# Row maximum in twelve one-bank parts, and a new order inside the attention chunk

## What is computed

```python
xn = _layernorm(x, axis=-1)
# attention: x 4 x 1024 x 128, 16 heads of 64
normed = xn / l2 * dim ** 0.5 * gamma
qkv = (normed @ w_qkv).reshape(b, n, 3, h, d)
sim = jnp.einsum('bhid,bhjd->bhij', q * d ** (-0.5), k)
sim = jnp.where(causal_mask, mask_value, sim)
attn = jax.nn.softmax(sim, axis=-1)
out = jnp.einsum('bhij,bhjd->bhid', attn, v)      # then @ w_out
# experts: top 2 of 8, relu(xn @ W1 + b1) @ W2 + b2, weighted, then layer_norm(xn + sum)
x = x + attention(xn) + experts(xn)
```

## Time and profile before

| | value |
|---|---|
| median of three runs | 1487.04 us |
| the profiled execution | 1485.95 us, span 1484.2 us |
| TensorE busy | 1396.8 us (94%) |
| VectorE busy | 1104.8 us (74%) |
| ScalarE busy | 1058.7 us (71%) |
| GpSimd busy | 947.7 us (64%) |
| attention stage | from about 262 us to the end |
| TensorE waits for row_max at L1271, all of the run | 20.8 us |
| TensorE waits for p_lo at L1313, all of the run | 1.3 us |
| one exponential (L1075), mean | 490 ns |
| VectorE's reductions (L1123), all 512 | 385.9 us |
| mean granted clock of TensorE | 0.975 |

### The profile page before, as it was taken

How to read it: one execution, slowest core, us unless ns; L and a number is a source line. 1 busy time by engine, 2 the same in 40 slices (tenths; PEclk the granted TensorE clock), 3 DMA queues, 4 the chain that set the end, 5 groups by cost and what they waited for, 6 DMA issues and landing times.

```text
span 1484.2 us, 27052 instructions
## 1 busy us (share of the span) xinstructions
PE 1396.8 (94%) x8618; PEld 1069.1 (72%) x8618; DVE 1104.8 (74%) x1928; ACT 1058.7 (71%) x2589; POOL 947.7 (64%) x933
## 2 busy tenths in 40 slices
PE   3689999599999999999999999999999999999996
PEld 3679999367777777777777777777777777777774
DVE  6645555458876987698769876987688768876985
ACT  2556666377777777777777777777777777777774
POOL 1774000168667866786678667866786678667775
PEclk9689999799999999999999999999999999999998
DMA  9122221122212221221122212221212121212112
GB/s 328 63 89 64 68 58 51 39 49 53 49 44 59 53 51 43 59 55 47 44 62 53 50 41 63 51 49 43 63 51 49 44 62 50 49 44 62 50 44 75
DMA packets 77226, 89.89 MB, mean 61 GB/s; under 512 B 17656, under 2 KB 54816, under 8 KB 77088
## 3 DMA queue, kind: packets, MB, share of 16 engines
q1 hardware_dynamic: 59168, 69.90, 18.6%
q10 hardware_dynamic: 13824, 9.86, 2.1%
q0 software_dynamic: 4096, 8.40, 2.0%
HBM read 37.25 MB, written 16.78 MB: 36 GB/s over the span
## 4 chain that ended last, share of the span: by engine, by line
PE 58%; DVE 11%; POOL 6%; issue 4%; ACT 2%; DMA 1%; SPq 0%; POOLq 0%
PE max_ps L1271 9%; PE head_ps L1313 7%; PE head_ps L1315 7%; PE head_ps L1317 7%; PE score_ps L1297 7%; PE score_ps L1296 6%; DVE row_max L1123 4%; POOL p_lo L1037 4%; PE misc_ps L1247 3%; PE misc_ps L1327 3%; POOL two_y L1030 2%; PE max_ps L1274 2%; PE misc_ps L1241 2%; PE score_ps L1299 2%; PE misc_ps L1243 2%
## 5 line engine op out<-in xcount | busy, mean ns | idle before, releaser
L1037 POOL TENSOR_TENSOR p_lo<-probs,p_hi 128x512 fp32r<-128x512 f32 (+3 forms) x768 | 805.5, 1068 | 322.5 <-ACT p_hi L1075 317.5
L1075 ACT ACTIVATE probs<-score_ps 128x512 f32<-128x512 f32 (+3 forms) x768 | 376.5, 490 | 211.8 <-PE score_ps L1299 116.7
L1123 DVE TENSOR_REDUCE row_max<-max_ps 128x1 f32<-128x128 f32 (+7 forms) x512 | 385.9, 754 | 174.0 <-PE max_ps L1274 169.0
L1075 ACT ACTIVATE p_hi<-score_ps 128x512 fp32r<-128x512 f32 (+3 forms) x768 | 375.3, 489 | 0.0
L1313 PE MATMUL head_ps<-p_hi,v_hi 128*65 128x512 f32 (+3 forms) x768 | 289.3, 377 | 2.2 <-POOL p_lo L1037 1.3
L1271 PE MATMUL max_ps<-k_a,q_a 128*128 128x384 f32 (+5 forms) x768 | 259.8, 393 | 26.2 <-DVE row_max L1123 20.8
L1296 PE MATMUL score_ps<-q_a,k_a 128*128 128x512 f32 (+3 forms) x768 | 266.5, 347 | 2.5 <-DMA q_b<-shift 2.5
L1297 PE MATMUL score_ps<-q_b,k_b 65*128 65x512 f32 (+3 forms) x768 | 267.7, 349 | 0.0
L1317 PE MATMUL head_ps<-p_lo,v_hi 128*65 128x512 f32 (+3 forms) x768 | 258.8, 337 | 0.0
L1315 PE MATMUL head_ps<-p_hi,v_lo 128*64 128x512 f32 (+3 forms) x768 | 258.7, 337 | 0.0
L1296 PEld LDWEIGHTS score_ps<-q_a,k_a 128*128 128x128 f32 x768 | 144.9, 189 | 45.2 <-issue 3.4
(11 more groups left out here) (162 smaller groups left out, 2193.6 us busy)
## 6 DMA issues: line engine op xcount, KB each, us to landing
k_a<-k_a SPq DMA_DIRECT2D x64, 256.0 KB, 4.0
q_b<-q_a SPq DMA_DIRECT2D x64, 256.0 KB, 4.8
scale<-inv_rows SPq DMA_DIRECT2D x128, 128.0 KB, 2.9
sorted_x<-zeros SPq DMA_DIRECT2D x13, 384.0 KB, 16.4
sorted_y<-result ACTq DMA_DIRECT2D x78, 64.0 KB, 1.7
w_raw<-sorted_x SPq DMA_DIRECT2D x25, 192.0 KB, 2.5
acc<-in_L_attn_x_dram SPq DMA_DIRECT2D x4, 512.0 KB, 6.9
w_raw<-in_L_ffn_W_dram ACTq DMA_DIRECT2D x1, 2048.0 KB, 23.2
```

Source lines behind the costliest of these rows:

```text
L1037: pool.tensor_tensor(p_lo[:, slot, 0:w], probs[:, n_chunk(g, c) % PROBS, 0:w], p_hi[:, slot, 0:w].bitcast(F32), ALU.subtract).then_inc(p_s ...
L1075: ins = act.activation(p[:, n_chunk(g, c) % ring, 0:width], score_ps[n_chunk(g, c) % 2][:, 0:width], ACT.Exp, scale=SCALE)
L1123: dve.tensor_reduce(row_max[:, g % 2, t:t + 1], src, axes, ALU.max).then_inc(max_taken, 1)
```

## The change

- The row maximum of a head comes in twelve parts, each in one bank, one part a chunk. A wide tile is two parts of half its width, whose results go to two columns of `row_max` (now `TILES + GROUP` wide). After the last part one small `tensor_tensor` maximum joins the four pairs (`max_merged`), and the shift of the second half waits for that. Part m waits for the reduction of part m - 2.
- Inside a chunk the order is: score, the first two weighted products, the maximum, the third weighted product (`pv_low`), then projection, `y` and shift. Before, it was score, maximum, projection, `y`, shift, and all three weighted products. The first two now wait for `probs_ready` (ScalarE), the third for `p_split` (GpSimd).
- `PROJECT_AT`, `COMBINE_AT`, `Y_AT` and the tables of the first head are moved to suit.
- The last step of a combine waits for the additions of `y` before it.
- In the expert stage TensorE keeps the expert's number of a tile in its register instead of reading it again two steps later.

```diff
@@ expert stage, TensorE
-                            inside = i is not None
-                            e_out = tile_experts[k - 2] if inside else expert_of(pe, j - 2)
+                            e_out = tile_experts[j - 2]
@@ tables
-            row_max = sb(ph2, "row_max", [P, 2, TILES])
+            row_max = sb(ph2, "row_max", [P, 2, TILES + GROUP])
-            max_parts = [(0, 0), (1, 1), (2, 0), (3, 1), (7, None), (6, None), (5, None), (4, None)]
-            MAX_AT = [0, 1, 2, 3, 5, 7, 10, 11]
-            FIRST_WIDE = {0: (4, 5), 1: (6,), 2: (7,)}
-            FIRST_MAX_AT = [3, 4, 5, 6, 7, 8, 9, 10]
+            max_parts = [(t, 0, (t + 1) * P, True) for t in range(4)]
+            for t in (7, 6, 5, 4):
+                w = (t + 1) * P // 2
+                max_parts += [(t, 0, w, False), (t, w, w, True)]
+            MAX_AT = {c: (c,) for c in range(CH)}
+            FIRST_WIDE = {0: (4, 5, 6), 1: (7, 8, 9), 2: (10, 11)}
+            FIRST_MAX_AT = {3: (0, 1), 4: (2,), 5: (3,), 6: (4, 5), 7: (6,), 8: (7, 8), 9: (9, 10), 10: (11,)}
-            BEFORE = [-1, -1, 0, 1, 3, 4, 5, 6]
-            HALF_MAX = [3, PARTS - 1]
+            NARROW = 4
-            PROJECT_AT = [{1: 0, 2: 1, 3: 2, 5: 3, 6: 4, 10: 5}, {}]
+            PROJECT_AT = [{1: 0, 2: 1, 4: 2, 5: 3, 6: 4, 9: 5}, {}]
-            COMBINE_AT = [(g, c) for g in (3, 4, 5, 6, 7) for c in (0, 1, 4, 6, 8, 9, 10, 11)][:COMBINE_STEPS]
-            Y_AT = {11: 0, 22: 1}
+            COMBINE_AT = [(g, c) for g in (3, 4, 5, 6, 7) for c in (0, 1, 3, 7, 8, 9, 10, 11)][:COMBINE_STEPS]
+            Y_AT = {11: 0, 17: 1}
@@ beside(at)
+                values = at >= LAG and (at - LAG) // CH < ALL_HEADS
+                if values:
+                    order.append(("pv", (at - LAG) // CH, (at - LAG) % CH))
                 max_at = MAX_AT if g else FIRST_MAX_AT
                 if g + 1 < ALL_HEADS and c in max_at:
-                    order.append(("max", g + 1, max_at.index(c)))
+                    order += [("max", g + 1, m) for m in max_at[c]]
+                if values:
+                    order.append(("pv_low", (at - LAG) // CH, (at - LAG) % CH))
...
-                if at >= LAG and (at - LAG) // CH < ALL_HEADS:
-                    order.append(("pv", (at - LAG) // CH, (at - LAG) % CH))
@@ VectorE, maximum(g, m)
-                        t, bank = max_parts[m]
+                        t, k0, w, _ = max_parts[m]
+                        to = t + GROUP if k0 else t
                         dve.wait_ge(max_scores, n_max(g, m) + 1)
...
+                        dve.tensor_reduce(row_max[:, g % 2, to:to + 1], max_ps[:, m % 2, 0:w], AX_X,
+                                          ALU.max).then_inc(max_taken, 1)
+                        if m == PARTS - 1:
+                            dve.wait_ge(max_taken, n_max(g, m) + 1)
+                            dve.tensor_tensor(row_max[:, g % 2, GROUP:TILES], row_max[:, g % 2, GROUP:TILES],
+                                              row_max[:, g % 2, TILES:TILES + GROUP], ALU.max).then_inc(max_merged, 1)
@@ VectorE, last step of combine
+                            if added[0]:
+                                dve.wait_ge(y_added, added[0] + 2)
@@ TensorE, max_scores_of(g, m)
+                        if n_max(g, m) >= 2:
+                            pe.wait_ge(max_taken, n_max(g, m) - 1)
+                        ins = pe.matmul(max_ps[:, m % 2, 0:w], q_a[i][s][:, t * P:(t + 1) * P],
+                                        k_a[i][s][:, k0:k0 + w], start=True, stop=not diagonal)
+                        if diagonal:
+                            ins = pe.matmul(max_ps[:, m % 2, w - P:w], later[:], ident16[:], start=False, stop=True)
@@ TensorE, shifts(g, half, u)
-                        pe.wait_ge(max_taken, n_max(g, HALF_MAX[half]) + 1)
+                        if half:
+                            pe.wait_ge(max_merged, g + 1)
+                        else:
+                            pe.wait_ge(max_taken, n_max(g, NARROW - 1) + 1)
@@ TensorE, values(g, c), and the new low_values(g, c)
-                        pe.wait_ge(p_split, n_chunk(g, c) + 1)
+                        pe.wait_ge(probs_ready, n_chunk(g, c) + 1 + 2)
...
+                    def low_values(g, c):
...
+                        pe.wait_ge(p_split, n_chunk(g, c) + 1)
                         pe.matmul(head_ps[0:HEAD + 1, cols], v_hi[i][:, j, s], p_lo[:, slot, 0:width],
                                   start=False, stop=c in LAST).then_inc(pv_done, 1)
```

More of the change, by code:

```diff
@@ L736, in attention_and_experts @@
         max_taken = sem("max_taken")
+        max_merged = sem("max_merged")
         misc_ready = sem("misc_ready")
@@ L904, in attention_and_experts @@
             order = [(kind, 0, n) for n in range(6) for kind in ("project", "project_lo")]
-            order += [("max", 0, m) for m in range(HALF_MAX[0] + 1)] + [("shift", 0, 0)]
+            order += [("max", 0, m) for m in range(NARROW)] + [("shift", 0, 0)]
             for at in range(ALL_HEADS * CH + 2 * CH):
@@ L1084, in _ @@
                             shifts(g, c, u)
-                        elif kind == "pv" and c in LAST:
+                        elif kind == "pv_low" and c in LAST:
                             half = LAST.index(c)
@@ L1116, in maximum @@
                     def maximum(g, m):
-                        t, bank = max_parts[m]
+                        t, k0, w, _ = max_parts[m]
+                        to = t + GROUP if k0 else t
                         dve.wait_ge(max_scores, n_max(g, m) + 1)
[L1119 to L1123, removed]
+                        dve.tensor_reduce(row_max[:, g % 2, to:to + 1], max_ps[:, m % 2, 0:w], AX_X,
[4 more added lines that the diff above has]
+                                              row_max[:, g % 2, TILES:TILES + GROUP], ALU.max).then_inc(max_merged, 1)
                     summed = [0]
+                    added = [0]
                     def combine(hp, part):
@@ L1188, in add_y @@
                                           acc[:, toks], ALU.add).then_inc(y_added, 1)
+                        added[0] += 1
                     dve.sem_inc(pv_done, RING)
@@ L1252, in max_scores_of @@
                         i, s = g // 2 % 2, g % 2
-                        t, bank = max_parts[m]
+                        t, k0, w, diagonal = max_parts[m]
                         if m == 0 and s == 0:
@@ L1316, in values @@
                                   start=False, stop=False)
+                    def low_values(g, c):
+                        half, j, q0 = chunks[c]
+                        i, s = g // 2 % 2, g % 2
+                        width = (half + 1) * BANK - q0
+                        slot, cols = (g * CH + c) % RING, slice(q0, (half + 1) * BANK)
+                        pe.wait_ge(p_split, n_chunk(g, c) + 1)
                         pe.matmul(head_ps[0:HEAD + 1, cols], v_hi[i][:, j, s], p_lo[:, slot, 0:width],
@@ L1341, in _ @@
                             values(g, c)
+                        elif kind == "pv_low":
+                            low_values(g, c)
                         elif kind == "y":
```

## The result

The changed kernel takes 1499.24 us, the median of four runs (1498.15 to 1500.89), against 1487.01 before. The ratio is 1.0088, with a 95% interval of 1.0067 to 1.0109: slower by 12 us, where 1455 was forecast. Its profiled execution took 1498.15 us, 12.2 more than that of before.

A forecast was written before the change was run, and what follows sets the result against it. TensorE's own time was taken to bound the attention stage, VectorE second. From 1485.95 us, 26 for 7.5 periods of eight heads and 5 for the experts were subtracted, giving 1455; range 1430 to 1480.

The forecast's parts named there:

- The load order: TensorE, attention heads: narrow products get narrower loads behind them, saving 0.55 us per even and 0.30 per odd head.
- rival B: TensorE in attention: reordering weight loads gives nothing, only head 6 falls, to 22.1 us; total 1476; chance 0.18.
- The expert stage: TensorE no longer rereads the expert's number in 78 steps: 0.06 us a step, 5 us, between 0 and 6.
- VectorE's share: VectorE per head: split reductions add 0.63 us, small maximum 0.5; in all 1.15, between 0.8 and 1.85.
- The waits: TensorE waiting in attention: head 6's wait goes, VectorE's lag partly remains; eight heads take 144.1 us, saving 3.5.
- Moving combine, projection and output steps: Attention heads' step tables: changes no sum; the output projection waits only if VectorE lags over some 2.5 us.
- The shift's chain: Row-maximum transpose in chunks 0 and 8 to its score product: nothing lost, 0.9 us of cover.
- C: Rival, slower: VectorE sets heads 3, 4 and 6 and keeps its idle time; total 1507 us; chance 0.12.

## Why the prediction was wrong

**The load order** was right. The floors came out at 19.74 and 15.35 us, for 20.0 and 15.2. An even and an odd head save 0.81 and 0.17 against 0.55 and 0.30 forecast, 0.98 a pair against 0.85; so the pair is right and its split is not. By itself it is worth 19 us, which puts rival B out: under it, the order alone would have given nothing.

**The expert stage** was right in kind and too small: steps take 2.14 us in place of some 2.24, the stage is 7.4 us shorter, and the register alone gives 9 us in the total, where 5 was taken and 6 was the bound. Some 2 us of the 9 are less half clock in the first head, as the register's own run shows. The bound failed because the transposes behind a copy can start earlier than the quick step of the earlier trace rows showed: 0.12 us after it, for 0.15. These are two neighbouring steps of the changed kernel, with the copy of the first:

```profile
170.56 0.69 DVE L604 COPY w_raw<-bank 128x512 f32<-128x512 f32 x1
...
171.37 0.60 PE L707 MATMUL bank<-ident,w_raw 128*128 128x128 f32 x4
...
173.50 0.60 PE L707 MATMUL bank<-ident,w_raw 128*128 128x128 f32 x4
```

**VectorE's share** holds the step that failed. The split reductions were a little cheaper than said: 417.9 us in 768 against 385.9 in 512, 0.50 us a head for 0.63. The small maximum was put at 0.5 us, with one whole subtraction of GpSimd, 1.07, as the upper end. It took 1.1 us on average and 3.75 at most. The upper end was wrong because it took for granted that the small maximum is let in after one subtraction. In most places it is: outside head 2's end it takes 0.73 us on average. At the end of head 2 it isn't: it is held through three whole subtractions and ends with the last of them. Besides, 1.07 is the mean over four widths; in the kernel before, a subtraction of 512 columns lasts 1.30. The Trainium skill (SBUF — State Buffer, Who interferes with whom) has the rule that bears on it: an operation of VectorE with two SBUF inputs contends with one of GpSimd that reads SBUF, and `tensor_reduce` never does on trn2. The runs agree, with 161 to 3746 ns against 160 to 165. I had cited the lock in the prediction and taken too small a price from it.

**The waits.** The wait of head 6 went, as said: that head takes 20.71 us, for 21.8 forecast. A new one came at the transpose of chunk 0, where the prediction looked for it, but in 40 heads of 64 and for 37.4 us: 2.04 us in head 3, 0.54, 0.77, 0.85 and 0.38 in heads 2, 4, 6 and 7. The second mistake is here. I gave the small maximum's price to VectorE's total and then let TensorE's slack absorb most of it, head by head. But the operation lies on the shift's chain. Between the last reduction and the moment when TensorE reaches the transpose there are 1.9 us in head 3 and none in head 4, and what the operation takes beyond that is TensorE's at once. VectorE's free time doesn't help: it had 28 us in eight heads before, and has 22 after. The four short falls of the clock behind head 3's wait, 6 us, weren't in the sum at all.

**Moving combine, projection and output steps** was said to change no sum. It costs 6 to 7 us in the twelve-part kernel. Which of the three tables does it was not tried.

**The shift's chain** itself was priced right: with the one-operand maximum added to it in eight parts, it costs nothing.

**The rivals.** C was on the right side, with the wrong place and a wrong reason for the size: its head 6 at 24.5 us came out at 20.71, and its head 2 at 20.6 came out at 21.83. The chance of 0.12 for C was too low for an operation that the trace of before didn't show and that stood on a chain.

**The rest of the sum.** With the second operand gone the changed kernel takes 1463.4 us, 8 above 1455. That it comes so near is partly luck, because two errors cancel. These are heads 2 and 4 and the sum of that kernel's eight heads:

```profile
609.37:631.23 21.86, 20.55 (x129) 15.06 (x127) 18.03 (x29) 17.75 (x40) 20.74 (x21) 1.00 0.34 83
...
646.58:668.88 22.30, 20.59 (x128) 14.86 (x127) 21.55 (x38) 17.87 (x40) 13.66 (x14) 1.00 0.32 76
...
sum 146.04, PE 142.27 PEld 104.75 DVE 124.41 ACT 114.82 POOL 107.92; mean PE 17.78 PEld 13.09 DVE 15.55 ACT 14.35 POOL 13.49
```

Forecast were 20.1, 20.8 and 144.1. In head 2 TensorE waits 1.1 us for GpSimd's subtractions, a wait that the prediction put at nothing; in head 4 it waits 1.7 for VectorE. The heads behind the first gain 12 us in all, where 26 were taken. On the other side, the first score product comes 9.3 us earlier and the first head is 2.1 shorter, where 5 were taken.

## What to carry to other kernels

A tiny VectorE operation with two SBUF inputs costs what GpSimd is doing, not its own size: here the rest of a subtraction in most places, and three whole ones in a row in one. Where something waits for it, use a form with one SBUF input (a reduction over a strided view, or an operand in PSUM), or keep it off the chain. Where two weight loads differ in width, put the narrow load behind the narrow product; that was worth 19 us here with no instruction saved. An operation that the trace doesn't show yet deserves a price in its worst place, one place at a time, before it is averaged over the program.

## What the runs showed of the hardware

Pauses of TensorE in the middle of dense work are sometimes followed by a short fall of its clock. Head 3 of the period that begins with head 8 in the changed kernel has the same instructions as the head 3 above (17.54 us at 1.00), and takes 19.07:

```profile
490.88:509.95 19.07, 17.04 (x101) 12.29 (x100) 15.04 (x24) 11.04 (x27) 12.53 (x13) 0.91 0.05 16
```

A clock of 0.91 over this stretch is 1.2 GHz instead of 2.4 for 3.4 us. It happened in four of the eight heads 3 of that run, each behind the 2.1 us pause, and cost 1.5 us each, 6 of the 12 us. In the kernel with two operands added it happened in six of eight, and there head 3 takes 16.36 us without the operand, 18.14 with it and 19.71 with the clock's fall too. With one operand there is no such pause and no fall between the stage's start and its end. So of the 33.7 us between those two kernels some 9 are the clock's, and 23 the wait. With the gathers moved there is no such pause either, and yet the clock falls in two of the eight periods, in head 2, amid waits of 0.52, 0.95 and 0.81 us. Why the same pauses have it in some periods and not in others stays open.
